# Two-stage MLP kernel: x of tiles 7 to 18 turned by VectorE through a DRAM bounce, with eight row slots and the loads moved

## The reference

```python
for e in range(4):
    g = silu(h @ Wg[e].T); u = h @ Wu[e].T; y = (g * u) @ Wd[e].T   # Wg = Wu = Wd = ctx_2048
    out = where(expert_ids == e, y, out)
x = x + tanh(g_xattn) * out
g = (h2 @ gate_w.T) * gate_s;  u = (h2 @ up_w.T) * up_s            # h2 = layernorm(x)
x = x + tanh(g_ffn) * ((silu(g) * u) @ down_w.T) * down_s
```

## Time and profile before

| | |
|---|---|
| median of 3 runs | 385.54 us (385.04 to 385.70) |
| profiled execution | 384.71 us, span 382.6 us |
| TensorE busy | 364.2 us, 95% of the span |
| VectorE, ScalarE, POOL busy | 244.6, 147.5, 92.5 us |
| expert stage, from the first turn of h (20 us) to 135.5 us | TensorE busy 112.0 of 115.5 us |
| second MLP, 135.5 us to the end | TensorE busy 240.7 of 247.1 us |
| granted clock of TensorE | 0.997 over the span |

### The profile page before, as it was taken

The page is one execution under the profiler, slowest core; times in us unless marked ns, Lnnn a source line. Parts: engine busy times, 40 slices in busy tenths (PEclk is TensorE's granted clock), DMA queues, the critical chain, the costliest instruction groups (busy, mean ns, idle before and its releaser), DMA issues.

```text
span 382.6 us, 5569 instructions
## 1 busy us (share of the span) xinstructions
PE 364.2 (95%) x1704; PEld 298.0 (78%) x1704; DVE 244.6 (64%) x451; ACT 147.5 (39%) x266; POOL 92.5 (24%) x131
## 2 busy tenths in 40 slices
PE   3899999997999999999999999999999999999993
PEld 2478888786888878888888888888888888888892
DVE  6877666767998878779856256647346757323353
ACT  3466565646654536323322222322222322222230
POOL 7497454343461220011003110002201001300022
PEclk9999999999999999999999999999999999999998
DMA  6768876756654246432301412301232310200002
GB/s 224 274 217 259 260 275 195 261 142 222 218 165 142 84 140 192 140 86 57 82 0 55 169 55 83 82 0 55 76 119 69 95 27 27 82 0 0 0 29 86
DMA packets 27281, 45.39 MB, mean 119 GB/s; under 512 B 2928, under 2 KB 13168, under 8 KB 27264
## 3 DMA queue, kind: packets, MB, share of 16 engines
q1 hardware_dynamic: 22912, 30.83, 25.8%
q0 software_dynamic: 4352, 14.35, 10.4%
HBM read 30.59 MB, written 14.57 MB: 118 GB/s over the span
## 4 chain that ended last, share of the span: by engine, by line
PE 85%; DVE 6%; DMA 5%; issue 2%; POOL 1%; SPq 0%; ACT 0%; DVEq 0%; POOLq 0%
PE bank L1283 41%; PE bank L1178 21%; PE bank L1290 20%; DMA turned_rows<-xn 2%; PE bank L1193 2%; DMA rows<-x,gidx 2%; PE bank L1157 1%; DMA xq<-turned_rows 1%; PE bank L1147 0%; DVE rows L1060 0%; DMA ids_i<-ids 0%; DVE tmp L1053 0%; DVE parts L808 0%; DVE bn L763 0%; DVE xn L1053 0%
## 5 line engine op out<-in xcount | busy, mean ns | idle before, releaser
L1283 PE MATMUL bank<-work,wgu 128*128 (+1 forms) x736 | 167.3, 380 | 0.1
L1283 PEld LDWEIGHTS bank<-work,wgu 128*128 128x128 f32 x736 | 133.9, 188 | 27.1 <-issue 0.5
L1178 PE MATMUL bank<-work,parts 128*128 (+1 forms) x432 | 106.3, 397 | 2.0 <-ACT parts L522 1.7
L1178 PEld LDWEIGHTS bank<-work,parts 128*128 128x128 f32 x432 | 79.0, 188 | 18.8 <-issue 2.4
L1290 PE MATMUL bank<-work,hp 128*128 128x512 f32 x352 | 87.3, 390 | 0.2 <-DVE hp L1019 0.2
L1290 PEld LDWEIGHTS bank<-work,hp 128*128 128x128 f32 x352 | 65.7, 188 | 14.4 <-DVE hp L1019 0.6
L1000 DVE SCALAR_TENSOR_TENSOR sh<-bank,gs,sh 128x512 f32<-128x512 f32 x42 | 31.5, 749 | 55.4 <-PE bank L1283 55.4
L630 ACT ACTIVATE hp<-sh 128x512 fp32r<-128x512 f32 x42 | 26.6, 632 | 78.5 <-DVE sh L1000 78.5
L625 ACT ACTIVATE sh<-bank,gs 128x512 f32<-128x512 f32 x42 | 28.9, 688 | 72.0 <-PE bank L1283 71.2
L496 POOL DMA_INDIRECT out<-rows x16 | 16.2, 1011 | 128.3 <-DVE rows L1060 105.8
L1006 DVE TENSOR_TENSOR hp<-sh,hp 128x512 fp32r<-128x512 f32 x42 | 29.0, 691 | 22.3 <-ACT hp L630 22.3
(11 more groups left out here) (134 smaller groups left out, 267.8 us busy)
## 6 DMA issues: line engine op xcount, KB each, us to landing
wraw<-guT SPq DMA_DIRECT2D x8, 704.0 KB
turned_rows<-xn SPq DMA_DIRECT2D x20, 256.0 KB
rows<-x_rows SPq DMA_DIRECT2D x8, 528.0 KB, 4.5
ctx_in<-ctxT SPq DMA_DIRECT2D x4, 1024.0 KB, 5.5
rows<-turned_rows SPq DMA_DIRECT2D x12, 256.0 KB
checked<-dwT SPq DMA_DIRECT2D x11, 256.0 KB
rows<-dwT SPq DMA_DIRECT2D x11, 256.0 KB, 2.8
xq<-turned_rows SPq DMA_DIRECT2D x8, 256.0 KB
```

What stands on the lines that cost most here:

```text
L1178: mm = pe.matmul(out_ps[:, :], part(s)[:, c * P:(c + 1) * P], ctx_w(e, c, w), start=n == 0, stop=n == last)
L1283: mm = pe.matmul(out_ps[:, tiles.start * P:tiles.stop * P], wgu[:, row + h, w, c * P:(c + 1) * P], moving, start=n == 0, stop=n == last)
```

## The change

`RING` becomes 8, of which two slots (`far`) lie in the second MLP's x buffer, `ON_PE` becomes 7, and the gather is five tiles ahead. From tile 7 on x goes through `tmp`, the norm of tile k + 3 is in step k (`norm(6)` and `norm(7)` are both in step 4), and `stats` is in one piece ahead of `hidden`. The four `first_stats` go to steps 10 to 13, one each. The stores count on two semaphores in turn, and each wait names the tile that it means. On SP, weight rows 3, 4 and 5 follow each other without check rows; check rows 4 to 10, the two `load_half` and weight rows 6 and 7 are issued between a bounce's write and its read. ScalarE waits for the store of tile 13 before it writes where that tile lay. Cut to its core:

```diff
-RING = 6
-ROWS = RING + BLOCK
+RING = 8
+NEAR = 6
+ROWS = NEAR + BLOCK
...
-ON_PE = 11
+ON_PE = 7
...
-    return (k + 4) % RING
+    return (k + 2) % RING
...
+        far = nc.alloc_sbuf_tensor_at("far", [P, RING - NEAR, 6 * D], F32, offset=work_base + CTX_WORDS * 4)
...
+        def tile_stored(k):
+
+            return stored[k % 2], 16 * (k // 2 + 1)
...
             weight_row(3)
-            check_row(4)
             weight_row(4)
             sp.wait_ge(S["ctx_lo"], len(ON_VECTOR))
             sp.wait_ge(S["pool_ctx_lo"], len(ON_POOL))
+            weight_row(5)
+
             def load_half(b, half_):
                 t = BLOCK * b + 2 * half_
                 at = row_slot(b, 2 * half_)
                 if b == 0:
-                    sp.wait_ge(S["stored"], 16 * (t + 2 + EXPERTS - 1))
+                    for k in range(t + EXPERTS - 1, t + EXPERTS + 1):
+                        sp.wait_ge(*tile_stored(k))
                 sp.dma_start(rows[:, at:at + 2, :], x1_v[:, t:t + 2, :])\
                   .then_inc((S["rows_a"], S["rows_b"])[half_], 16)
 
-            for r in range(5, 2 * KC):
-                check_row(r)
-                weight_row(r)
-            load_half(0, 0)
-            check_row(8)
+            def loads_between(n):
+
+                if 1 <= n <= 7:
+                    check_row(n + 3)
+                if n in (4, 6):
+                    load_half(0, n // 2 - 2)
+                if n in (8, 9):
+                    weight_row(n - 2)
 
             def turn_rows(n):
 
                 sp.wait_ge(S["xn_ready"], n + ON_PE + 1)
                 sp.dma_start(turned[n].rearrange("i p c -> p i c"),
-                             xn[:, :].rearrange("p (i c) -> p i c", i=QUADS)).then_inc(S["xn_out"], 16)
+                             (tmp if n < AHEAD else xn)[:, :].rearrange("p (i c) -> p i c", i=QUADS))\
+                  .then_inc(S["xn_out"], 16)
+                if n < AHEAD:
+                    loads_between(n)
                 sp.wait_ge(S["xn_out"], 16 * (n + 1))
                 if n:
                     sp.wait_ge(S["xt_ready"], n)
                 sp.dma_start(quarter_rows(n < AHEAD),
                              turned[n].rearrange("i (a g) c -> (i a) (g c)", g=QUADS)).then_inc(S["xq_in"], 16)
 
-            turn_rows(0)
-            load_half(0, 1)
-            check_row(9)
-            turn_rows(1)
-            check_row(10)
-            for n in range(2, AHEAD):
+            for n in range(AHEAD):
                 turn_rows(n)
             for c in range(IC):
                 if c < 4:
-                    sp.wait_ge(S["stored"], 16 * (TILES + c))
+                    sp.wait_ge(*tile_stored((11, 16, 17, 18)[c]))
                 else:
                     sp.wait_ge(S["down_lo"], c - 3)
                 sp.dma_start(rows[:, down_slot(c), 0:D], dw_v[c]).then_inc(down_landed[c % 4], 16)
...
+            gather(6)
+            token_in(6)
             for k in range(2, STEPS + 1):
-                if k < ON_PE:
+                if k <= ON_PE - 3:
                     inverse_std(k + 2)
+                if ON_PE - 3 <= k < STEPS - 3:
+                    inverse_std(k + 3)
                 if k == NORM_AT:
                     first_inverse_std()
-                pool.wait_ge(S["stored"], 16 * (k - 1))
-                if k + 4 < STEPS:
-                    gather(k + 4)
-                    token_in(k + 4)
-                if ON_PE - 1 <= k < STEPS - 3:
-                    inverse_std(k + 3)
+                if k > 2:
+                    pool.wait_ge(*tile_stored(k - 3))
+                if k + 5 < STEPS:
+                    gather(k + 5)
+                    token_in(k + 5)
...
             step(16)
+            act.wait_ge(*tile_stored(13))
             first_x_hi(1)
...
                 if m >= ON_PE:
                     x_in = x_in.rearrange("p (c i b) -> p c i b", c=KC, i=QUADS)
-                    x_out = x_out.rearrange("p (i c b) -> p c i b", c=KC, i=QUADS)
+                    x_out = tmp[:, :].rearrange("p (i c b) -> p c i b", c=KC, i=QUADS)
                 if m > ON_PE:
                     dve.wait_ge(S["xn_out"], 16 * (m - ON_PE))
-                elif m:
+                elif 0 < m < ON_PE:
...
             def step_on_pe(k):
                 h_lo(k - 1)
-                norm(k + 1, ring_slot(k + 1))
+                norm(k + 1)
                 landed(k + 2)
-                stats(k + 2, ring_slot(k + 2))
+                stats(k + 2, ring_rows(k + 2)[:, :, 0:D])
                 hidden(k)
                 x_lo(k + 1)
+                if k == ON_PE - 3:
+                    norm(k + 2)
+                    landed(k + 3)
+                    stats(k + 3, ring_rows(k + 3)[:, :, 0:D])
                 update(k - 1)
+                if k == ON_PE - 3:
+                    norm(k + 3)
 
             def last_on_pe(k):
 
                 h_lo(k - 1)
-                norm(k + 1, ring_slot(k + 1))
-                landed(k + 2)
-                stats(k + 2, ring_slot(k + 2))
+                landed(k + 3)
+                stats(k + 3, ring_rows(k + 3)[:, :, 0:D])
                 hidden(k)
                 x_lo(k + 1)
-                norm(k + 2, ring_slot(k + 2))
+                norm(k + 3)
                 update(k - 1)
-                landed(k + 3)
-                stats(k + 3, ring_slot(k + 3))
-
-            def step(k):
+
+            def step(k, block_row=None):
                 h_lo(k - 1)
-                if k + 2 < STEPS:
-                    norm(k + 2, ring_slot(k + 2))
-                if k + 1 > ON_PE:
-                    turn(k + 1 - ON_PE, True)
-                hidden(k)
-                if k + 1 == ON_PE:
-                    turn(0, True)
+                turn(k + 1 - ON_PE, True)
                 if k + 3 < STEPS:
                     landed(k + 3)
-                    begin_stats(ring_slot(k + 3))
+                    stats(k + 3, ring_rows(k + 3)[:, :, 0:D])
+                hidden(k)
                 turned_lo(k + 1)
                 if k + 3 < STEPS:
-                    end_stats(k + 3)
+                    norm(k + 3)
+                if block_row is not None:
+                    first_stats(block_row)
                 update(k - 1)
 
...
             for k in range(EXPERTS, ON_PE - 2):
                 step_on_pe(k)
-            first_stats(0)
-            first_stats(1)
             last_on_pe(ON_PE - 2)
-            for k in range(ON_PE - 1, NORM_AT):
-                step(k)
-                if k % 2:
-                    first_stats((k - STATS_AT) // 2 + 2)
+            for k in range(ON_PE - 1, 14):
+                step(k, k - STATS_AT if k >= STATS_AT else None)
```

More of the change, by code:

```diff
@@ L211, in token_half, with ring_rows, ring_row, token_of @@
             return slice(i * D // 2, (i + 1) * D // 2)
-        def token_of(first, last):
-            return rows[:, first:last, D:D + 1].bitcast(U32)
+        def ring_rows(k, count=1):
+            at = ring_slot(k)
+            return rows[:, at:at + count, :] if at < NEAR else far[:, at - NEAR:at - NEAR + count, 0:WIDE]
+        def ring_row(k):
+            return ring_rows(k)[:, 0, 0:D]
+        def token_of(b, t):
+            return rows[:, row_slot(b, t), D:D + 1].bitcast(U32)
         def first_xt(i):
@@ L246, in quarter_rows @@
         def quarter_rows(expert=False):
-            return xq0[:, :] if expert else rows[:, RING - 2, 0:D]
+            return xq0[:, :] if expert else rows[:, NEAR - 2, 0:D]
         def turned_x(expert=False):
-            return xt0[:, :] if expert else rows[:, RING - 1, 0:D]
+            return xt0[:, :] if expert else rows[:, NEAR - 1, 0:D]
         def ctx_w(e, c, s):
@@ L271, in build @@
         down_landed = [sem(f"down_landed{n}") for n in range(4)]
+        stored = [sem(f"stored{n}") for n in range(2)]
         last_stored = [sem(f"last_stored{t}") for t in range(BLOCK)]
+        def tile_stored(k):
+            return stored[k % 2], 16 * (k // 2 + 1)
         def hold(eng):
@@ L449, in _ @@
             gather(3)
-            pool.wait_ge(S["pads"], 1)
-            token_in(0, 2)
-            token_in(2, 4)
+            pool.wait_ge(S["pads"], 2)
+            token_in(0, 4)
+            token_in(4, 2)
             inverse_std(1)
@@ L756, in store_table, with stats, begin_stats @@
                    .then_inc(S["tables_ready"], 1)
-            def stats(m, at):
-                begin_stats(at)
+            def stats(m, row):
+                begin_stats(row)
                 end_stats(m)
-            def begin_stats(at):
-                dve.bn_stats(bn[:, 0, :], rows[:, ds(at, 1), 0:D]).then_inc(S["bn_parts"], 1)
+            def begin_stats(row):
+                dve.bn_stats(bn[:, 0, :], row).then_inc(S["bn_parts"], 1)
             def end_stats(m):
@@ L801, in first_norm @@
                     dve.wait_ge(S["xt0_done"], t)
-                dve.tensor_scalar((tmp, xn)[t // (BLOCK - 1)][:, :], rows[:, row_slot(0, t), 0:D],
+                else:
```

(25 more changed lines are left out.)

37 lines of the change are left out of this document (18 added, 19 removed).

## The result

| | before | after |
|---|---|---|
| median of 20 runs | 385.80 us | 384.31 us |
| lowest and highest | 384.82, 393.75 | 382.08, 386.98 |
| profiled execution's span | 382.6 us | 380.8 us |

The ratio is 0.9955 with a 95% interval of 0.9937 to 0.9973: the change makes the kernel faster by 1.0 to 2.4 us. The prediction said 4.93 us less and a range from 379.6 to 383.2. The direction was right, the size was not, and the time lies 1.1 us above the range.

The account below looks back on a forecast made before the run. TensorE was taken to bound the kernel. Turns removed 1.94 plus stalls removed 3.69, less 0.5 for the prologue and 0.2 for the new passage, gave 4.93 us off 385.54: 380.6 us, range 379.6 to 383.2.

Parts of the forecast that it names:

- What bounds the kernel: Whole kernel: TensorE owns 85% of the chain, so time counts only where its work moves or it stands still.
- the turns: Expert stage, tiles 7 to 10: their x turns leave TensorE, 0.49 us each, saving 1.94 us.
- the stalls: Three long steps at the old passage from TensorE turns to DRAM bounces become ordinary, saving 3.69 us.
- The prologue: First product of tile 3: gather(6) ahead of the power for tile 4 costs 0.3 to 0.65 us, 0.5 taken.
- The new passage: First bounce, at tile 7: write landed 53.3, turn at 56.0; nearly nothing lost, 0.2 us taken, bounds none and 2.5.
- Rival B: First bounce late: row 5 goes out before the first write, whose completion comes behind it; 382.6 us, chance 0.21.
- Rival C: Starting a pipeline of bounces costs 3.69 us wherever it starts, at tiles 6 to 8; 384.1 us, chance 0.12.
- Loads between write and read: Bounces with SP loads: 7.9 us available for 5.4, or 7.5 with 704 KB; covered, 0.4 to 2.5 us spare.
- Steady steps: VectorE's list takes 5.02 us against 5.92; 6.03 with statistics in steps 10 to 13, drifting some 0.5 us, nothing lost.

Follow-up runs that it names:

- turns_back: Changed kernel with TensorE turning x up to tile 10 again, weight and check rows alternating, tile 6's gather behind the power for tile 4; 382.78 us.
- row4_held: Changed kernel with weight row 5 between the fourth bounce's write and read, SP still waiting for row 4's landing before the first write; 381.83 us.
- row5_late: Changed kernel with weight row 5 loaded between the fourth bounce's write and read instead of ahead of the first write; 383.34 us.
- best_again: Second run of the changed kernel with weight row 5 after the fourth read and tile 6's gather behind the power for tile 4; 381.78 us.
- best: Changed kernel with weight row 5 after the fourth bounce's read and tile 6's gather behind the power for tile 4; 381.56 us.

## Why the prediction was wrong

- **What bounds the kernel, the turns, the stalls:** right. The turns were worth 1.94 (1.72 to 2.02 by turns_back), the old passage 3.69 (3.63). The x turns fell from 40 matmuls to 24, and VectorE's rose to 12 of 1087 ns.
- **The prologue:** right in mechanism and place, forecast 0.3 to 0.65 with 0.5 taken, measured 0.37. The row behind it was POOL's gather of 1.03 to 1.35 us; this one took 0.99. (The latest end of the power adds up to 35.42, not 35.45.)
- **The new passage:** the step that failed. "Nearly nothing lost; I take 0.2", with 2.5 as its bound; measured 2.77 and 2.13. Two terms of it were too small. Row 4 was to land near 48 and landed at 50.32, 6.42 us after it could go out, at 43.90: at 48 to 50 us the DMA engines are busy for 0.06 of their time (26 GB/s), so most of the traffic was over and some last part of that load was late. I had taken the time when traffic ended for the time when a load lands. And the write behind row 5 took 5.35 where I took 4.88 from the earlier trace rows. Together 2.8 us later than reckoned (56.1 instead of 53.3; 2.4 from the start of step 4, which comes 0.38 later in the new trace), on a slack of 0.05 us at the turn of h. The other mistake was to choose: a term with no slack, that hangs on two DMA landings of 4 to 6 us each, was given 0.2 as its likeliest value, next to its best case.
- **Rival B** (0.21) is what happened: row 5 went out ahead of the first write, which landed after 55.3. Its price of 1 us for each us late holds: in the four traces with this order on VectorE the write lands 14.2, 14.6, 14.6 and 15.2 us after the start of step 4 and step 6 loses 1.81, 1.98, 2.13 and 2.77. That its time, 382.6, still lies 1.7 under the measured one is the larger loss, 2.77 against 2, the scatter behind the last store, and the higher median before. By the rule of the Trainium skill cited there ("DMA: Bandwidth & Descriptors", Queues, rings and completion order) the write's completion comes after row 5's writes. No trace shows when row 5 landed, but the write's 5.35 to 6.27 us with it in front are in line with that. The landing is late too where the load is issued 0.4 us behind the write (5.05 to 5.65 us), which an order after earlier writes alone doesn't give.
- **Rival C** (0.12) gave nearly the measured time, 384.1, for a wrong reason: row4_held and turns_back start the pipeline for nothing.
- **Loads between write and read:** "covered, with 0.4 to 2.5 us to spare" was half right. In the kernel after no step was long for it. But I had 2.64 us for the write whatever stands behind it, and with 704 KB issued 0.4 us behind it took 5.05 to 5.65; a read issued 2.5 to 2.8 us behind row 5 took 5.6 (row5_late, row4_held), where I had 4.9. The slack was used up in 4 traces of 10, by 0.24 to 1.39 us.
- **Steady steps:** right in the time: 5.92, and no long step from 10 to 13 in the kernel after. VectorE's list with statistics takes 5.91 from start to start (the low halves of h at 87.20 and 93.11) where I had 6.03, so there was no drift to hide.
- **The size of the whole:** the profile gave 1.8 us less, the medians 1.5, the ratio 1.7. Against the profile's 1.8 the prediction's 4.93 us is 2.6 too much by the passage and 0.7 by what follows the last store's issue, which I hadn't in the sum and which is scatter. The range ended at 383.2 with 2.5 us for the passage (by the sum it would be 382.9); 2.77 instead, that scatter, and a median before that is 0.26 higher over 20 runs than over the 3 that I had, put the time above it.

## What to carry to other kernels

When work moves to a chain that goes through DRAM, look first at what its first transfer finds in front of it: here one weight row, put early because its buffer was free, took back 2.8 of 5.6 us, and moving that one line and one gather gave the rest. Keep large loads off a write or read that an engine waits for on both sides, ahead and right behind, and issue them after a read whose next write is still some 2 us off (row 5 after the fourth read: that next write took 3.9 to 4.2 us; row 6 only 0.5 us ahead of one: 5.6). And where a step of a sum has slack near zero between two DMA landings, its likeliest value is a loss of the usual spread of a landing, not nothing.

## What the runs showed of the hardware

- **A write to DRAM of 256 KB lands some 1.5 to 3 us later with a 704 KB load near it, on either side of it.** From its issue to that of the read that waits for it: 2.3 to 3.0 us for the last five tiles of the expert stage in the kernel before, which have none of SP's loads near them (2.64 in the earlier trace rows; its first took 3.85), 3.3 to 3.4 for the first bounce of the kernels with row 5 moved, and 3.6 to 3.95 in turns_back, again with none of SP's loads near. With the load 0.4 to 0.5 us ahead 5.35 to 6.27 (six writes), with it 0.4 us behind 5.05 to 5.65 (ten). Issued 0.8 to 1.0 us behind, the spread is wide, 3.4 to 6.3. Why the times without a load differ by over 1 us no run here takes apart.
- **A load can land 2 us after the traffic has all but stopped.** Weight row 4 landed at 50.32, in the kernel after. The window over 48 to 50 us has a DMA share of 0.06, which is as much as one of 16 engines at work:

```profile
48.00:50.00 2.00, 2.00 (x11) 1.61 (x10) 1.94 (x4) 1.71 (x4) 1.65 (x4) 1.00 0.06 26
```

  Which ones and why no run here shows; in row4_held row 4 had landed before the write was ready.
- **One load in the prologue spreads the executions by some 2 us.** ScalarE's timeline in the kernel before and in best_again, at the same instructions:

```profile
17.36 1.15 ACT L509 ACTIVATE work<-ctx_in 128x512 fp32r<-128x512 f32 x2 [1.78 <-DMA ctx_in<-ctxT]
```

```profile
19.25 1.15 ACT L531 ACTIVATE work<-ctx_in 128x512 fp32r<-128x512 f32 x2 [3.73 <-DMA ctx_in<-ctxT]
```

  The third expert's weights landed 1.9 us later there, and step 2 started at 30.12 instead of 27.76. Over the 14 traces that start lies between 27.75 and 30.12, and the five in which ScalarE got these weights after 18.9 have the five latest starts, from 29.57 on; `best` and best_again, the same kernel, have 27.82 and 30.12, and spans of 377.5 and 379.8. It is one reason why differences of under 1 us are plain in the steps and lost in the medians.
